# GpSimd's register waits ahead of the pacing wait in the gather of a two-layer graph network

## The reference

```
scores = where(A != 0, -arange(N), -inf)
vals, idx = top_k(scores, 25)
agg = x[idx].max(axis=neighbours)              # limits by the degree
x1  = layernorm(x + relu([x, agg] @ W + b))
w   = leaky_relu(e_src[i] + e_dst[j])  where A[i, j] != 0
y   = relu(softmax(w) @ h + bias) + h          # per head, then a norm per head
out = layernorm(x1 + norm(y))
```

## Time and profile before

| | us |
|---|---|
| median of 3 runs | 5611.73 (5609.56 to 5616.21) |
| the profiled execution | 5598.51 |
| its span, first to last instruction | 5596.7 |
| DVE busy | 3947.8 (71%) |
| POOL busy | 3855.2 (69%) |
| PE busy | 3722.0 (67%) |
| ACT busy | 2181.3 (39%) |

### The profile page before, as it was taken

The page is one execution under the profiler, slowest core; times in us unless marked ns, Lnnn a source line. Parts: engine busy times, 40 slices in busy tenths (PEclk is TensorE's granted clock), DMA queues, the critical chain, the costliest instruction groups (busy, mean ns, idle before and its releaser), DMA issues.

```text
span 5596.7 us, 60889 instructions
## 1 busy us (share of the span) xinstructions
PE 3722.0 (67%) x12546; PEld 1650.0 (29%) x12546; DVE 3947.8 (71%) x12445; ACT 2181.3 (39%) x4674; POOL 3855.2 (69%) x6404
## 2 busy tenths in 40 slices
PE   2232267667676767777777777677777766777787
PEld 1111133323323333333333233323323332333232
DVE  4444477777777777777777777777777777777666
ACT  3333334334444434444443444444344443433212
POOL 5777777777777777777777777777777777777300
PEclk8555577777777777767777777777777777777888
DMA  3333334434334443443444444344444443443100
GB/s 123 116 114 121 114 123 125 131 124 128 123 120 128 130 128 124 128 126 119 129 125 130 125 127 124 122 127 131 128 123 128 125 133 115 133 124 110 54 23 27
DMA packets 264414, 658.87 MB, mean 118 GB/s; under 512 B 62161, under 2 KB 128978, under 8 KB 247762
## 3 DMA queue, kind: packets, MB, share of 16 engines
q0 software_dynamic: 153600, 419.64, 25.9%
q1 hardware_dynamic: 110546, 236.66, 12.1%
HBM read 605.73 MB, written 50.33 MB: 117 GB/s over the span
## 4 chain that ended last, share of the span: by engine, by line
POOL 59%; issue 22%; PE 9%; DVE 7%; ACT 1%; DMA 1%; POOLq 1%; SPq 0%; DVEq 0%; another core or an unknown queue 0%; ACTq 0%
POOL rows L495 53%; POOL idle L498 6%; PE acc L1258 6%; DVE uv L837 2%; DVE rmax L856 1%; DMA rows<-in_x_dram,idx 1%; PE pB L1226 1%; PE rq L1196 1%; PE acc L1184 1%; DVE top L724 1%; ACT raw L574 0%; PE pA L1213 0%; DVE key_b L726 0%; PE pB L1227 0%; POOLq L491 0%
## 5 line engine op out<-in xcount | busy, mean ns | idle before, releaser
L495 POOL DMA_INDIRECT rows<-in_x_dram,idx x3200 | 3469.2, 1084 | 1380.8 <-POOL idle L498 971.4
L1258 PE MATMUL acc<-uv,hs 128*65 128x512 f32 x4096 | 2195.1, 693 | 79.2 <-ACT raw L574 58.8
L837 DVE SCALAR_TENSOR_TENSOR uv<-rq,qinv,maskT 128x512 f32<-128x512 f32 x2048 | 1502.9, 740 | 614.6 <-PE acc L1258 281.4
L1258 PEld LDWEIGHTS acc<-uv,hs 128*65 128x65 f32 x4096 | 629.0, 161 | 1357.2 <-issue 1316.4
L856 DVE TENSOR_TENSOR rmax<-rmax,rows 128x1280 f32<-128x1280 f32 x384 | 570.7, 1486 | 530.6 <-DMA rows<-in_x_dram,idx 530.3
L1236 PE MATMUL pA<-id,xh 128*128 128x128 f32 x256 | 87.4, 444 | 920.7 <-DVE xh L819 906.9
L648 ACT ACTIVATE x1T<-pA 128x256 f32<-128x256 f32 x128 | 49.1, 383 | 1239.3 <-PE pA L1236 1239.3
L639 ACT ACTIVATE xaT<-pA 128x512 f32<-128x512 f32 x128 | 76.4, 597 | 1049.8 <-PE pA L1213 916.3
L1226 PE MATMUL pB<-w_sb,xaT 128*128 128x256 f32 x1024 | 363.2, 517 | 113.5 <-DVE pad L739 67.7
L498 POOL MEMSET idle<- 128x8 f32 x3200 | 385.8, 121 | 2.6
L1236 PEld LDWEIGHTS pA<-id,xh 128*128 128x128 f32 x256 | 36.7, 202 | 1023.3 <-DVE xh L819 1006.9
(11 more groups left out here) (117 smaller groups left out, 4699.4 us busy)
## 6 DMA issues: line engine op xcount, KB each, us to landing
adj_sb<-in_adj_dram SPq DMA_DIRECT2D x128, 1024.0 KB
rows<-in_x_dram,idx POOLq DMA_INDIRECT x3200
xh_dram<-xh SPq DMA_DIRECT2D x128, 256.0 KB
xr<-xh_dram SPq DMA_DIRECT2D x64, 512.0 KB
xt<-in_x_dram SPq DMA_DIRECT2D x128, 128.0 KB
out_dram<-xr SPq DMA_DIRECT2D x32, 512.0 KB
w_sb<-in_L_gnn_W_dram SPq DMA_DIRECT2D x1, 512.0 KB
wcat<-in_L_gnn_W_dram SPq DMA_DIRECT2D x2, 128.0 KB
```

Source lines behind the costliest of these rows:

```text
L495: nc.gpsimd.indirect_dma_start(rows[:, c, r * C:(r + 1) * C], None, x_rows, bass.IndirectOffsetOnAxis(ap=idx[u][:, k:k + 1], axis=0)).then ...
L837: stt = nc.vector.scalar_tensor_tensor(uv[k][:, i, :], rq[i][:], inv, m, ALU.max, ALU.mult)
L1258: last = nc.tensor.matmul(acc[i][0:HW, :], hs[:, (1 - quad.par) * JT + jt, h, :], uv[k][:, i, :], start=(jt == 0), stop=(jt == JT - 1))
```

## The change

In each tile GpSimd's register arithmetic, its wait for `s_rfree` and the increment of `s_go` come ahead of the wait for the last memset; likewise the wait for the indices at the start of a tile. The wait for the memset stands right before the indirect DMA. For that, `s_pace` counts on over the four tiles of a quad, from 1 to 100, and is cleared once, at the quad's end, after a wait for 100. The first indirect DMA of a quad has no pacing wait of its own.

```diff
                 for v in quad.reach(lambda q: QT * q + u + 1):
                     pool.wait_ge(s_idx, v)
-                pace = Chain(pool, s_pace)
                 for c in range(CH):
                     for v in quad.reach(lambda q: CH * (QT * q + u) + c + 1):
                         pool.wait_ge(s_rfree, v)
                         pool.sem_inc(s_go["pool"], 1)
                     for r in range(CR):
                         k = c * CR + r
+                        paced = u * S + k
+                        if paced:
+                            pool.wait_ge(s_pace, paced)
                         nc.gpsimd.indirect_dma_start(
                             rows[:, c, r * C:(r + 1) * C], None, x_rows,
                             bass.IndirectOffsetOnAxis(ap=idx[u][:, k:k + 1], axis=0)).then_inc(s_rows[c], 16)
-                        pace.then(nc.gpsimd.memset(idle[:], 0.0))
-                pace.end()
+                        nc.gpsimd.memset(idle[:], 0.0).then_inc(s_pace, 1)
+                if u == QT - 1:
+                    pool.wait_ge(s_pace, QT * S)
+                    pool.sem_clear(s_pace)
```

## The result

The changed kernel takes 5182.0 us (median of 4 runs, 5177.06 to 5184.95) against 5612.14 (5609.56 to 5616.21) for the kernel before: ratio 0.923, 95% interval 0.9216 to 0.9244. Forecast were 5287.0 us in a range of 5230 to 5410. The direction was right and the gaps closed as forecast, but the gain was larger than the whole range: 430 us by the medians, 413.6 by the spans (5596.7 to 5183.1). The 16 us between them are where the two profiled executions lie: the one before is 13.2 us under the median of its first runs, the one after 3 us above its own.

What follows compares the result with a forecast made beforehand. POOL's own string of gathers, memsets and gaps was taken as the bound. Gains of 57 + 26 x 9.9 + 11 = 325 us off the profiled 5598.5 gave 5273.5, plus 13.2 for the median: 5287, range 5230 to 5410.

Steps and rivals of the forecast that it cites:

- the term that carries it: POOL's chunk and tile starts: sequencer work hides behind running DMA and memset, gaps fall to 0.27, 382 us off.
- Quad starts: POOL at a quad's start: wait for 100, clear and loop branch stay as before, so 0 gain.
- the long idles: 33 idles of 1.6 us on POOL, each 95 indirect DMAs after the last: number of DMAs stays, so 0 gain.
- C: POOL's semaphore instruction runs in order, only the memset signal's 0.27 overlaps: about 185 us gained, 5427; chance 0.08.
- D: POOL's sequencer stops until its engine is empty: nothing hides, gaps stay, 5612 us; chance 0.05.
- B: PE and VectorE give back half in the steady part: 211 us gained, 5401; chance 0.09.
- E: Denser descriptor writing by POOL collides with VectorE at lines 495 and 856: slower, 5665 us; chance 0.04.
- I put both at 1.9 us a quad: 11.8 - 1.9 = 9.9: Steady quads: uneven tiles and VectorE's longer waits for PE take 1.9 us a quad, leaving 9.9 gained.
- The 150.7: VectorE's steady quad without its waits for rows, in us: 162.5 less 11.8.
- some 7% more of them hit: 30 us, about 0.9 a quad: POOL's DMAs: its busy share rises 7%, so more are blocked by VectorE's instructions, costing 30 us.
- the gain is whole: 57: First 5 quads, before 850 us: POOL alone sets the pace, so 3 x 10.9 + 2 x 12.1 = 57 us gained.
- the 382 less a few: The range's fast end: nearly all 382 us of shortened POOL gaps gained; 5612 - 382 = 5230.

Runs made afterwards that it cites:

- the second trace: The changed kernel once more, unaltered, as the control of an undisturbed set (TensorE's signals not late): 5178.16 us, ratio 0.9238.
- The two experiments from either side: Against the changed kernel: half the columns of later `uv` products left out, 5119.33 us; two pacing semaphores used in turn, 5163.04 us (both in undisturbed sets).
- the kernels with one part of the change: Against the kernel before, the new wait order at inner chunk starts only: 5267.73 us (0.9381); at tile starts only: 5498.15 us (0.9807).
- the 6060 us: The changed kernel itself, unaltered, third time, in a set where TensorE's signals came late: 6060.25 us, ratio 1.08.

## Why the prediction was right or wrong

Right: **the term that carries it.** "If the sequencer can pass them while memset and DMA run, the gap falls to 0.27": it does, 382 us forecast, 379 measured, at chunk and tile starts, in loops and written out. Quad starts and the long idles stayed. Rivals C and D fall by these gaps, B by VectorE's waits for PE of 417 us in the steady part (`rq` and the ring of `uv`, as it counted them), E by a mean gather of 1071 ns. Waits of POOL for the maxima were to appear; they rose from 14.4 to 17.3 us only. The last gather was to start near 4920 and started at 4820.

Wrong, first: **"I put both at 1.9 us a quad: 11.8 - 1.9 = 9.9".** This made VectorE the bound of the steady part, with 150.7 + 1.9 = 152.6 us a quad. The quad is 150.50, and without its waits for rows VectorE's is 149.5 (148.6 in the second trace). The two experiments from either side found POOL's string the bound. POOL's own quad was put at 151.3, 0.8 too high, since its blocking was put 1.2 too high and the rest 0.4 too low. By POOL alone the prediction had 11.2, so this step cost 26 x (11.2 - 9.9) = 34 of the 88.6 us by which the forecast missed the span. The idea that VectorE's other waits grow was not the fault, as the traces without late signals show (1 to 3 us). The 150.7 under it was too high: in the kernels with one part of the change a quad without the waits for rows is 146.2 and 147.6 us. The likely reason is that the trace of the kernel before has late signals; a second trace of it, without them, was not taken.

Wrong, second, and the costliest: **"some 7% more of them hit: 30 us, about 0.9 a quad".** Blocking fell by 41 us. In the steady part it stayed, 13.37 and 13.09 a quad, and the 0.9 a quad that were taken off there cost 23 us. In quads 0 to 3 it went from 51.5 to 23.9, in quad 4 from 12.0 to 9.6, and that is the difference between "the gain is whole: 57" and 87.0. The argument took the hits as random in time and their cost as fixed. Where VectorE waits for rows neither holds: 63 gathers are hit before and after, but the maximum starts at a fixed distance from the gathers, and the change moved them, from a median of 0.47 us behind the maximum's start to 1.17. The delay at two places shows that with the new waits too.

Third, **the range.** Its lower end was the 382 less a few, so it left no room for a second gain; a bound on the blocking to either side, 28 us in four quads, would have brought it to 5202, still 20 above the result. Of the 105 us between forecast and result 88.6 are the span's and 16 are the place of the two profiled executions among their runs. Of the 88.6, 58 are the steady quads (34 the allowance, the rest nearly all blocking), 30 the first five, 3 the last, where blocking fell too (14.8 to 11.2), and -4 the tail.

The risk that no step named is the 6060 us. E was a slower case by contention on the port; what came was late signals, in a kernel whose two bounds lie within 1 to 2 us a quad. Why they cost this kernel 880 us and the one before nothing is not shown.

## What to carry to other kernels

A sequencer's waits and register work belong ahead of the wait for the engine's own last instruction: behind it each lays bare the preparation of the next instruction, here 0.6 us before an indirect DMA; in front it cost nothing here, as the buffers that it waits for had long been free. When two engines share a port and one of them waits for the other, their collisions are a phase: look at which starts first, and by how much, before a gap between them is changed. And before a wait of another engine goes into a sum, look whether its signals came in time in that trace. When the bounds of two engines nearly coincide, run the kernel on more than one chip before its time is believed: the same change was 7.7 and 7.6% faster in two sets and 8% slower in one.

## What the runs showed of the hardware that was not expected

- Two kernels with the same instructions on GpSimd, one delay of 0.28 us a chunk at another place, lie 134 us apart (5434 and 5301).
- A gather that starts inside a maximum ends 0.82 to 0.84 us after the maximum's end: all 63 of quads 0 to 3 do, before and after, from 0.13 to 1.31 us behind its start. One that starts 0.17 us ahead takes 0.95, and the maximum that it overlaps isn't lengthened.
- Increments by TensorE can reach the waiting engines several us after the matmul's end as the profile has it, in two of five sets (on some chips or after some kernels: open), with SyncE's issue of a load stretched from at most 368 ns to 1410. The kernel before showed nothing of it in its time, the changed one took 880 us longer.
